# Four graph layers on one core: in the first layer, the adjacency's loads issued from GpSimd's queue instead of the sync engine's

## What is computed

```python
node_att = softmax(x @ node_w, axis=0)
h = x @ edge_w
e = where(adj > 0, h @ h.T, -9e15)
edge_att = softmax(e, axis=1)
x = layernorm(x + (adj * (node_att * edge_att)) @ (x @ weight) + bias)
```

## Time and profile before

| | us |
|---|---|
| Median of 3 runs (lowest, highest) | 857.46 (856.97, 860.05) |
| The profiled execution, its own time | 860.67 |
| Its span, first to last instruction | 858.9 |
| TensorE busy | 788.6 (92%) |
| VectorE busy | 457.4 (53%) |
| ScalarE busy | 331.8 (39%) |
| GpSimd busy | 103.0 (12%) |

### The profile page before, as it was taken

How to read it: one execution, slowest core, us unless ns; L and a number is a source line. 1 busy time by engine, 2 the same in 40 slices (tenths; PEclk the granted TensorE clock), 3 DMA queues, 4 the chain that set the end, 5 groups by cost and what they waited for, 6 DMA issues and landing times.

```text
span 858.9 us, 12185 instructions
## 1 busy us (share of the span) xinstructions
PE 788.6 (92%) x4264; PEld 518.4 (60%) x4264; DVE 457.4 (53%) x956; ACT 331.8 (39%) x531; POOL 103.0 (12%) x200
## 2 busy tenths in 40 slices
PE   6868999999768999898997999999998999998997
PEld 5755766666466787777773654556654455465343
DVE  4574776667768668787874347212226021111655
ACT  3664655554136345454652214313335121222200
POOL 0010111111271001010101122000001100000343
PEclk9988999999879999999999999999999999999999
DMA  5669999998600000000002000000000000000011
GB/s 177 148 135 215 236 233 227 221 220 181 135 7 13 1 1 2 1 0 0 0 0 81 1 0 0 1 1 0 0 0 25 0 1 1 0 0 0 19 37 43
DMA packets 114870, 50.71 MB, mean 59 GB/s; under 512 B 103568, under 2 KB 109840, under 8 KB 114832
## 3 DMA queue, kind: packets, MB, share of 16 engines
q1 hardware_dynamic: 114832, 50.22, 26.7%
HBM read 22.95 MB, written 2.10 MB: 29 GB/s over the span
## 4 chain that ended last, share of the span: by engine, by line
PE 46%; issue 23%; SPq 13%; DMA 6%; ACT 4%; DVE 4%; POOL 4%; POOLq 0%; ACTq 0%; DVEq 0%
PE ps L631 10%; PE ps L751 10%; PE ps L729 8%; PE ps L779 7%; SPq L348 6%; SPq L341 5%; DMA adjf<-in_adj 4%; PE ps L760 3%; PE ps L716 3%; PE ps L519 2%; ACT adjb L816 2%; POOL x L461 2%; PE ps L542 1%; SPq L333 1%; DMA turned<-pl 1%
## 5 line engine op out<-in xcount | busy, mean ns | idle before, releaser
L631 PE MATMUL ps<-adjT,x 128*128 (+1 forms) x768 | 173.5, 379 | 7.9 <-DVE x L1299 4.2
L631 PEld LDWEIGHTS ps<-adjT,x 128*128 128x128 f16 x768 | 71.7, 98 | 93.2 <-issue 5.8
L572 PE MATMUL ps<-sup,turned 128*128 128x512 f16 x256 | 89.2, 396 | 11.5 <-DMA turned<-pl 10.7
L656 PE MATMUL ps<-H_hi,es_hi 128*128 128x258 f32 x256 | 76.3, 298 | 9.5 <-DVE es_lo L1040 6.0
L1040 DVE TENSOR_TENSOR hh_lo<-hf,hh_hi 128x512 fp32r<-128x512 f32 x32 | 22.2, 692 | 116.6 <-ACT hf L986 116.6
L751 PE MATMUL ps<-adjT,G 128*128 x384 | 83.6, 379 | 0.4 <-ACT hf L986 0.4
L656 PE MATMUL ps<-H_hi,es_lo 128*128 128x258 f32 x256 | 72.4, 283 | 0.0
L656 PE MATMUL ps<-H_lo,es_hi 128*128 128x258 f32 x256 | 72.3, 282 | 0.0
L574 PE MATMUL ps<-sup,turned 128*128 128x256 f16 x256 | 72.1, 282 | 0.0
L751 PEld LDWEIGHTS ps<-adjT,G 128*128 128x128 f16 x384 | 37.2, 98 | 45.4 <-issue 0.9
L887 ACT ACTIVATE es_hi<-tm 128x1024 fp32r<-128x1024 f32 x32 | 33.9, 1059 | 76.5 <-DVE tm L1217 63.2
(11 more groups left out here) (201 smaller groups left out, 1453.3 us busy)
## 6 DMA issues: line engine op xcount, KB each, us to landing
adjf<-in_adj SPq DMA_DIRECT2D x32, 512.0 KB, 5.7
x<-in_x SPq DMA_DIRECT2D x4, 512.0 KB, 7.9
out<-adjf SPq DMA_DIRECT2D x16, 128.0 KB, 1.7
adjf<-in_L_gnn_W SPq DMA_DIRECT2D x1, 1024.0 KB, 5.3
W1f<-in_L_gnn_W SPq DMA_DIRECT2D x1, 512.0 KB, 3.7
adjf<-in_L_gnn_W SPq DMA_DIRECT2D x1, 512.0 KB, 3.9
we<-in_L_gnn_edge_w SPq DMA_DIRECT2D x1, 256.0 KB, 3.8
w0x<-in_L_gnn_weight SPq DMA_DIRECT2D x1, 256.0 KB, 6.9
```

What stands on the lines that cost most here:

```text
L572: ins = mm(bank(6 + u), PT(HI, u)[:, jt, :], sup[:, jt, :], start=(jt == 0), stop=False, skip_group_check=True)
L631: ins = mm(bank(4 + f), x16[:, part, jt, f * P:(f + 1) * P], adj(b, jt), start=(jt == 0 and part == HI), stop=(jt == T - 1 and part == LO))
L656: ins = mm(bank(k, D + 2), es[p][:, jt % RE, k * P:(k + 1) * P], H[q][:, jt, :], start=(jt == 0 and (p, q) == (HI, HI)), stop=(jt == T - 1 ...
```

## The change

The loop of loads moves from the sync engine's block to GpSimd's, with the same waits, buffers and sizes. The sync engine keeps the first loads of x and the weights, and all transposes. GpSimd issues load 0 once x and the weights have landed, loads 1 to 3 ahead of its three reductions, loads 4 to 6 behind them and ahead of the first `bias_x`, and load t + 7 at the end of its round t.

```diff
--- before.py
+++ after.py
@@ -326,13 +326,6 @@
             sp.dma_start(w0x[:, :, D:D + 1], w_tiles(node_in)).then_inc(w0_landed, 16)
             sp.dma_start(brow[:, :], vec_row(b0_in)).then_inc(w0_landed, 16)
 
-            def load_adj(t):
-                for k in range(2):
-
-                    wait_from(sp, adj_cast, 2 * (t - 1) + k + 1)
-                    sp.dma_start(adjf[:, k, :], adj_in[t * P:(t + 1) * P, k * HALF:(k + 1) * HALF]) \
-                        .then_inc(adj_landed[k], 16)
-
             def turn_adj(t):
 
                 sp.wait_ge(adj_cast, 2 * t + 2)
@@ -347,29 +340,19 @@
                 wait_from(sp, pv_mm, t - 1)
                 sp.dma_start_transpose(PT(part, t % 2), (ph, pl)[part][:, :]).then_inc(PT_landed[part], 16)
 
-            load_adj(0)
-            load_adj(1)
-            turn_adj(0)
-            load_adj(2)
-            turn_adj(1)
-            load_adj(3)
-            turn_adj(2)
+            for t in range(3):
+                turn_adj(t)
             turn_p(0, HI)
             turn_p(0, LO)
+            turn_adj(3)
             turn_p(1, HI)
-            load_adj(4)
-            turn_adj(3)
-            load_adj(5)
             turn_p(1, LO)
             turn_adj(4)
             for t in range(2, T):
                 turn_p(t, HI)
                 turn_p(t, LO)
-                if t + 4 < T:
-                    load_adj(t + 4)
                 if t + 3 < T:
                     turn_adj(t + 3)
-
 
             sp.wait_ge(adj_cast, 2 * T)
             sp.dma_start(wsx[:, :, 0:D], w_tiles(wsa_in)).then_inc(wt1_landed, 16)
@@ -433,20 +416,33 @@
                 wait_from(pool, xb_used, before + t)
                 nc.gpsimd.tensor_tensor(xb[:, u, :], tile(x, t), brow[:, :], ALU.add).then_inc(xb_ready, 1)
 
-            pool.wait_ge(w0_landed, 48)
+            def load_adj(t):
+
+                for k in range(2):
+                    wait_from(pool, adj_cast, 2 * (t - 1) + k + 1)
+                    nc.gpsimd.dma_start(adjf[:, k, :], adj_in[t * P:(t + 1) * P, k * HALF:(k + 1) * HALF]) \
+                        .then_inc(adj_landed[k], 16)
+
             for c in range(B):
                 pool.wait_ge(x_landed[c], 16)
+            pool.wait_ge(w0_landed, 48)
+            for t in range(4):
+                load_adj(t)
             pool.wait_ge(node_max, 1)
             nc.gpsimd.partition_all_reduce(nst[:, 1:2], nst[:, 0:1], P, RMAX).then_inc(node_gmax, 1)
             pool.wait_ge(tmax_ready, 1)
             nc.gpsimd.partition_all_reduce(g1[:, 1:2], g1[:, 0:1], P, RMAX).then_inc(gmax_ready, 1)
             pool.wait_ge(node_exp, 1)
             nc.gpsimd.partition_all_reduce(nst[:, 4:5], nst[:, 3:4], P, RADD).then_inc(node_sum, 1)
+            for t in range(4, 7):
+                load_adj(t)
             bias_x(0, 0)
             bias_x(1, 1)
             for t in range(T - 2):
                 norm_factor(t, t % 2)
                 bias_x(t + 2, t % 2)
+                if t + 7 < T:
+                    load_adj(t + 7)
             norm_factor(T - 2, 0)
             norm_factor(T - 1, 1)
             pool.drain().then_inc(l0_done, 1)
```

## The result

The changed kernel takes **890.0 us** (median of 4 runs, 884.53 to 891.63) against 857.5: a ratio of 1.0371 [1.0335, 1.0407], 32 us slower. The prediction was 856.0, with a range up to 864. The profiled execution took 891.63, with a span of 889.8, 30.9 more than before. In after, L556 is the scores' matmul, L568 the weighted one, L334 and L341 are the transposes.

A forecast was written before the change was run, and what follows sets the result against it. TensorE, 92% busy, bounds the layer, so its waits at start and end count. Terms +4.9 - 3.2 - 2.4 - 1.3 + 0.5 = -1.5 us gave 856.0 against the median 857.46; range 849 to 864.

The forecast's parts named there:

- A round of it falls to three transposes of about 2.3 us, 7 us: Sync queue's rounds: without loads, three transposes take 7 us instead of 12.0, under TensorE's 10.7.
- First configuration, +11.3: Layer start: GpSimd's configuration for reductions, 8.44 us, now behind load 3, delays the first reduction from 47.17 to 58.4.
- S(2) to S(4), "without a wait and warm": Early layer: W(1) no longer waits and runs at full clock, cutting the lag from +11.3 to +4.9 us.
- Second configuration, 0: Behind load 6: `xb` ready at 96.5, final0(0) done at 97.6, just before W(2) at 97.7; no cost.
- Late gaps, -3.2: Late rounds: TensorE's waits for `pl`, 3.2 us, vanish as the sync queue's round gets shorter than TensorE's.
- the end, -2.4 and -1.3: Layer's end: LO(15) lands 2.4 us sooner, and W(15), after a shorter idle time, saves half of the slow clock's 2.7.
- Load t + 7 "right after" the cast of t + 6: GpSimd's rounds: load issued directly after that cast, landing in 6.7 us against a 10.7 us round; cost 0.
- the DMA engines are the limit: Rival: busy engines, not the queue, set the 5.13 us issue, so middle and end gains fail; 862.9, chance 0.12.

The follow-up runs named there:

- e3: Changed kernel with configurations hidden, transposes in the old order, and GpSimd's loads and the transposes waiting for each other's landing; 902.96 us (one run).
- e1: Changed kernel with loads 1 to 15 issued by ScalarE, load 0 by the sync engine, GpSimd as before the change; 873.22 us, ratio 1.0159.
- e7: Kernel before with only the first configuration for the reductions moved behind cast(2); 863.43 us, ratio 1.0071.
- e13: Kernel before with the change's loads 0 to 6 from GpSimd and both configurations late, turn_adj(3) behind LO(1); 874.63 us, ratio 1.0176.
- e8: Kernel before with only loads 6 to 15 issued by GpSimd, where the change puts them; 867.64 us, ratio 1.0119.
- e12: Changed kernel with loads 7 to 15 back in the sync queue, keeping its order turn_adj(3), HI(1), LO(1); 885.55 us, ratio 1.0312.
- e4: Changed kernel with load t + 7 ahead of bias_x(t + 2) in GpSimd's round instead of behind it; 887.62 us, ratio 1.0359.
- e10: Kernel before with loads 6 to 15 from GpSimd, second half placed behind the next row maxima; 865.63 us, ratio 1.0085.
- e11: Kernel before with loads 5 to 15 issued by ScalarE, halves meant to go apart; 856.91 us, ratio 0.9984.
- m1: Micro kernel without the layers: eight 512 KB transposes and eight 512 KB loads, issued at once; together 33.0 us (GpSimd's loads) and 34.4 us (ScalarE's).
- e14: Kernel before with GpSimd issuing loads 0 to 3 ahead of the first configuration, the rest as before; 868.84 us, ratio 1.0117.

## Why the prediction was wrong

- **The step that failed** is "A round of it falls to three transposes of about 2.3 us, 7 us". The 2.3 us were read from transposes with no load in flight, and I took the load as a thing of the queue: move it, and the transpose behind it is cheap. In this kernel a load in flight makes a transpose slow, also when another queue issued it: with the two kept apart (e3) the transposes are back at 1.3 to 3.5 us, and with ScalarE issuing the loads (e1) they still stall. In one queue the load meets one transpose in three, the adjacency's, for which nobody waits. From another queue it also meets HI and LO, whose landing TensorE waits for, and it stays in flight longer (7.1 us for 5.7). Medians of issue in after are 3.7 us for adjT, 3.6 for HI and 2.7 for LO, and from HI(3) at 117.73 to HI(12) at 225.74 a round of the queue takes 12.0 us, as long as with the loads in it, where I had 7. Against the sum, 18.7 us are lost up to S(4), 11.2 from there to the end of W(15), and 3.2 in the drain.
- **First configuration, +11.3**: the reduction started at 62.49, +15.3, and S(2) came 13.7 late. The configuration was right (8.13 for 8.44). What was missing came before it: load 3's second half was issued at 53.83 and not at 49, since cast(1) waited for its load (TensorE's longest wait for `smax` is 4.3 us instead of 0.8) where I allowed 0.5. The price of the configuration alone is e7's: +6, as its chain said (forecast 861 to 863, measured 863.4).
- **S(2) to S(4), "without a wait and warm"**: fell with the 2.3 us: W(1) waited 13.90 us. The stretch should have given 6.4 us back, and took 10.4 more. This is the largest part of the miss. e7 shows that with the loads in the sync queue the same chain gives back 5.4 us, nearly what was forecast.
- **Second configuration, 0**: right in the change, for the wrong reason. `xb` for tile 0 was ready at 113.65 and not at 96.5, and its cover wasn't the first configuration's lag but the late W(1). That the term came out was luck: e13 has the wait.
- **Late gaps, -3.2, and the end, -2.4 and -1.3**: the middle didn't gain 3.2; waits of 3.07, 4.66 and 0.67 us stand there. Moved alone (e8) it loses 10, 2.1 of them in the drain. Behind the late start it loses less: from e12 to the change it is 4.5, and from S(4) to the end of W(15) the change is 4.3 us longer than the kernel before. W(15) waited 3.31 us and ran warm, so there the step was right in direction.
- **Load t + 7 "right after" the cast of t + 6**: it stands behind `bias_x(t + 2)`, which waits a round longer. True, but e4 says that this costs nothing.
- **Not in the sum**: the drain at the layer's end, +3.2.
- **The rival "the DMA engines are the limit"** was the nearest to the truth, at 0.12, and too mild: it let the loss of the single queue persist, and had no term for two queues that make it larger. A share over 1 goes with 116 GB/s and with 248, so it tells little of what gets done. The range should have had a branch in which every transpose meets a load and takes the 5.13 us of the earlier trace rows: 15.4 a round against 10.7, which is outside of 864 by itself. Even that would have been a bound and no forecast, as the round measured 12.0.

## What to carry to other kernels

A transfer's duration read from a trace belongs to what was in flight beside it; before moving a transfer to another queue, ask which others it will now meet, and who waits for those. One queue with a good order is a schedule: it let each load slow the one transpose that nobody was waiting for. If a second queue is to help, issue its transfers singly and apart, try ScalarE before GpSimd, and keep transposes that an engine waits for out of their time; here the best of it was 0.4%. Look in the trace whether transfers that were to go apart did: in e10 and e11 they didn't. And a lag at the start of a pipeline can hide part of what goes wrong later, so that parts measured alone don't add up (27 for the start and 10 for the middle, 32 together).

## What the runs showed of the hardware

- The same 12 transposes and 8 loads took from 42.3 to 56.9 us, by who issues the loads and how far apart. The Trainium skill (DMA: Bandwidth & Descriptors, "Issuing engines are not separate DMA queues") says that DMAs issued from different engines run on the same 16 DMA engines and interleave, and that issuing from several saves issue time alone. The interleaving is there; that it saves or costs no more isn't what these runs show: against one queue beside them, a second one gave back 5.4 us in one rhythm (42.3 for 47.7) and cost 10.2 in another (56.9 for 46.7).
- Issued all at once, the loads of a second queue pass the transposes: a transpose stood for 13.0 and 15.7 us (m1). The Trainium skill (same page, "Queues, rings and completion order") has each DMA engine take turns between queues by whole packets. That would fit if its packets were those that the profile counts, of which 103568 of 114871 in after are under 512 bytes, the transposes' among them, while a load moves 4 KB a row; no run here shows that they are, or separates this from another cause, and it doesn't explain why the rate falls. That stays open.
- GpSimd's switch from the built-in operations to the reductions took 7.87 to 8.57 us in the six kernels that show it, and the first switch back 6.80 to 8.97, once 10.60. It wasn't prepared while GpSimd waited 14.04 us for a cast ahead of load 3. The Trainium skill (GPSIMD Engine Reference, Instruction dispatch) gives 5.95 us, measured, for the first call of a newly loaded kernel; all of these took longer.
- What the next layer's first matmul waited for GpSimd's drain grew with the number of load halves that its queue had issued: 3.6 us with 8 halves (e14), 4.1 with 14 (e12, e13), 4.6 and 5.5 with 20, 5.6 to 6.6 with all 32; without any it waited 3.4, once 4.4 (e11), for VectorE.
